# Two states of each unit take their product with B on GpSimd, and three positions per unit change who makes it

## What is computed

```python
dt = jax.nn.softplus(jnp.einsum('blr,dr->bld', x_dbl[..., :DT_RANK], dt_w) + dt_b)
Bm = x_dbl[..., DT_RANK:DT_RANK + D_STATE]
Cm = x_dbl[..., DT_RANK + D_STATE:]
dA = jnp.exp(dt[..., None] * A)
dBu = dt[..., None] * Bm[:, :, None, :] * u[..., None]
def step(h, ins):
    dA_t, dBu_t, C_t = ins
    h = dA_t * h + dBu_t
    y = jnp.einsum('bdn,bn->bd', h, C_t)
    return (h, y)
```

## Time and profile before

| | |
|---|---|
| median of 3 runs | 503.31 us |
| the profiled execution | 503.27 us, its span 501.5 us |
| first scan starts, last scan starts | 29.7 us, 466.3 us |
| busy: DVE, PE, ACT, POOL | 436.4, 421.1, 374.1, 370.7 us |
| scans (DVE) | 128, 290.4 us busy |
| products with B (DVE) | 92, 111.7 us busy |
| products with C (POOL) | 129, 301.2 us busy |
| mean granted TensorE clock | 0.912 of full speed |

### The profile page before, as it was taken

The page is one execution under the profiler, slowest core; times in us unless marked ns, Lnnn a source line. Parts: engine busy times, 40 slices in busy tenths (PEclk is TensorE's granted clock), DMA queues, the critical chain, the costliest instruction groups (busy, mean ns, idle before and its releaser), DMA issues.

```text
span 501.5 us, 6592 instructions
## 1 busy us (share of the span) xinstructions
PE 421.1 (84%) x2236; PEld 279.5 (56%) x2236; DVE 436.4 (87%) x357; ACT 374.1 (75%) x716; POOL 370.7 (74%) x226
## 2 busy tenths in 40 slices
PE   1947985999689897989899879999998977989754
PEld 1335654665445494555555676655645665558543
DVE  4577877999999987999999897999999788999454
ACT  2398799679959778999689786998687788684140
POOL 1799769577977797879688877878677977866521
PEclk9957988899999799999999797998999597799878
DMA  7242212212221222221122221222222122110001
GB/s 241 80 168 67 91 58 84 83 78 94 79 89 56 91 69 85 84 88 59 72 81 105 88 85 53 75 86 85 84 71 94 72 84 84 58 68 2 0 1 42
DMA packets 14721, 39.28 MB, mean 78 GB/s; under 512 B 1376, under 2 KB 5728, under 8 KB 14688
## 3 DMA queue, kind: packets, MB, share of 16 engines
q1 hardware_dynamic: 14688, 38.87, 22.2%
HBM read 37.55 MB, written 1.31 MB: 77 GB/s over the span
## 4 chain that ended last, share of the span: by engine, by line
DVE 24%; PE 24%; issue 20%; POOL 10%; ACT 7%; POOLq 0%; DVEq 0%; ACTq 0%
DVE bb L1072 11%; DVE hq L1084 10%; POOL hq L977 9%; PE ysum L618 8%; PE scr L729 3%; PE bb L599 3%; PE scr L697 2%; ACT da L784 2%; PE scr L660 2%; ACT g L871 2%; PE bb L572 1%; PE scr L750 1%; PE bb L750 1%; PE scr L555 1%; ACT ln_tile L888 1%
## 5 line engine op out<-in xcount | busy, mean ns | idle before, releaser
L977 POOL TENSOR_TENSOR hq<-hq,c_tiles 128x1024 f32<-128x1024 f32 x129 | 301.2, 2347 | 86.5 <-DVE hq L1084 86.5
L1084 DVE TENSOR_TENSOR_SCAN hq<-da,bb 128x1024 f32<-128x1024 f32 x128 | 290.4, 2281 | 22.3 <-PE bb L599 18.9
L784 ACT ACTIVATE da<-dt,neg_a 128x511 f32<-128x511 f32 x256 | 167.0, 712 | 24.2 <-DVE hq L1084 23.9
L618 PE MATMUL ysum<-wts,hq 128*128 128x128 f32 x1024 | 149.2, 293 | 4.3 <-POOL hq L977 4.1
L618 PEld LDWEIGHTS ysum<-wts,hq 128*128 128x128 f32 x1024 | 122.0, 149 | 28.9 <-issue 21.1
L1072 DVE TENSOR_TENSOR bb<-bb,dtu 128x1024 f32<-128x1024 f32 x92 | 111.7, 1214 | 8.8 <-PE bb L572 5.3
L871 ACT ACTIVATE g<-dtu_t,bc_t 128x256 f32<-128x256 f32 x144 | 61.0, 497 | 0.0
L599 PE MATMUL bb<-wts,g 128*128 128x128 f32 x288 | 41.8, 292 | 20.9 <-ACT g L871 19.5
L599 PEld LDWEIGHTS bb<-wts,g 128*128 128x128 f32 x288 | 34.3, 149 | 37.6 <-ACT g L871 23.5
L572 PE MATMUL bb<-b_rows,pick 48*128 48x512 bf16 x88 | 35.7, 406 | 16.0 <-DVE hq L1084 15.3
L572 PEld LDWEIGHTS bb<-b_rows,pick 48*128 48x128 bf16 x88 | 8.2, 94 | 52.9 <-DVE hq L1084 32.7
(11 more groups left out here) (123 smaller groups left out, 430.6 us busy)
## 6 DMA issues: line engine op xcount, KB each, us to landing
c_tiles<-c_rows_dram SPq DMA_DIRECT2D x64, 512.0 KB, 3.5
wconv<-conv_taps_dram SPq DMA_DIRECT2D x2, 512.0 KB, 7.3
x_res<-x_dram SPq DMA_DIRECT2D x1, 768.0 KB, 9.1
out_dram<-o SPq DMA_DIRECT2D x3, 256.0 KB, 2.3
wts<-packed_dram SPq DMA_DIRECT2D x1, 584.0 KB, 10.1
ffn_stage<-w_ffn_dram SPq DMA_DIRECT2D x1, 576.0 KB, 8.5
wts<-packed_dram SPq DMA_DIRECT2D x1, 437.0 KB, 7.0
x_res<-x_dram SPq DMA_DIRECT2D x1, 256.0 KB, 2.9
```

The costliest lines, as they stand in the source:

```text
L618: mm = nc.tensor.matmul(ysum[:, h, block(b)], hq[:, i % H_RING, h, block(b)], ident, start=(first and b == 0), stop=(i % NS == NS - 1), is ...
L784: ins = nc.scalar.activation(da[:, i % DA_RING, h, 1:SEQ], dt[:, k % 2, h, 1:SEQ], ACT.Exp, scale=neg_a[:, c:c + 1])
L977: nc.gpsimd.tensor_tensor(hq[:, i % H_RING, halves, :], hq[:, i % H_RING, halves, :], c_tiles[:, n % C_RING, i % 2, :].unsqueeze(1).broadc ...
L1084: nc.vector.tensor_tensor_scan(out=hq[:, i % H_RING].rearrange("p h t -> p (h t)"), data0=da[:, i % DA_RING].rearrange("p h t -> p (h t)") ...
```

## The change

A third kind of step is added, **pooled**, at positions 8 and 15 of a unit (15 alone in unit 0), 15 steps in all. Its dBu is made on POOL (stage "mul_b_pooled"): `dtu` times a row of B that SP has loaded, broadcast over the partitions, into `b_tiles` (a ring of 2, 256 KB per transfer). The result goes to `dbu`, one tile in SBUF. It is put behind mul_c of position 4 (for 8) and of position 12 (for 15), and waits for the scan of the last pooled step. For such a step ACT writes the decay not into `da` but into the `bb` tile in PSUM (stage "exp_psum"): one copy of the two zero columns and two exp instructions. This stage stands where the bcast of the step would stand, one slot ahead of the scan, and waits for scan i - 2, where the exp into `da` stood five slots ahead. The scan of the step reads the decay from PSUM and dBu from SBUF.

The table TURNED has other positions (33 turned steps in place of 36), so 80 plain steps are left of 92. The copies "g" are placed by a table, 3 to 5 slots ahead in place of 3; in the forward units from 2 on, dtu_turn and the "g" of the next unit's position 0 move one slot earlier. The buffer in DRAM now holds the rows of B too (32 rows per unit in place of 16). The staging tile for the feed-forward weights shares the memory of `hid`.

```diff
-TURNED = ((4, 6, 8, 10, 12, 14), (0, 3, 6, 9, 11, 13)) + 3 * ((6, 9, 12, 14), (0, 6, 9, 13))
+TURNED = ((4, 6, 10, 13), (0, 4, 6, 10, 13)) + 3 * ((3, 6, 10, 13), (0, 5, 10, 13))
+POOLED = ((15,),) + 7 * ((8, 15),)
+POOLED_RING = 2
...
+        g_slot = {3: 0, 4: 1, 5: 1, 6: 2, 10: 6, 13: 8 if ffn else 10}
         for p in TURNED[k]:
             if p:
-                put(at + p - 3, ("g", at + p))
+                put(at + g_slot[p], ("g", at + p))
+        for p in POOLED[k]:
+            put(at + {8: 4, 15: 12}[p], ("mul_b_pooled", at + p))
...
-            put(at + 12, ("dtu_turn", n, 0))
-            put(at + 13, ("dtu_turn", n, 1))
+            soon = 1 if d == 0 and k >= 1 else 0
+            put(at + 12 - soon, ("dtu_turn", n, 0))
+            put(at + 13 - soon, ("dtu_turn", n, 1))
...
-                put(at + 14, ("g", at + NS))
+                put(at + 14 - soon, ("g", at + NS))
...
-        return [("exp", n) for n in ahead.get(i, (i + DA_RING - 1,)) if n < STEPS]
+        return [("exp", n) for n in ahead.get(i, (i + DA_RING - 1,)) if n < STEPS and not is_pooled(n)]
...
-                order.append(("g_turn" if is_turned(i + 1) else "bcast", i + 1))
-            if i + 1 < STEPS and not is_turned(i + 1):
+                order.append(("g_turn" if is_turned(i + 1) else "exp_psum" if is_pooled(i + 1) else "bcast", i + 1))
+            if i + 1 < STEPS and not is_turned(i + 1) and not is_pooled(i + 1):
                 order.append(("mul_b", i + 1))
...
-                sp.dma_start(c_rows[k], xdbl[ROW_C:ROW_C + NS, :]).then_inc(s_cst, 16)
+                sp.dma_start(bc_rows[k], xdbl[0:2 * NS, :]).then_inc(s_cst, 16)
...
+                    for p in POOLED[k]:
+                        if m == {8: 0, 15: 3}[p]:
+                            n = pooled_steps(NS * k + p)
+                            if n >= POOLED_RING:
+
+                                sp.wait_ge(s_dbu_pooled, n - POOLED_RING + 1)
+                            sp.dma_start(b_tiles[:, n % POOLED_RING], bc_rows[k, ROW_B + p].partition_broadcast(P)
+                                         ).then_inc(s_bl[n % POOLED_RING], 16)
...
+                elif stage == "exp_psum":
+
+                    i, = a
+                    k, n = i // NS, i % NS
+                    act.wait_ge(s_scan, i - BB_RING + 1)
+                    nc.scalar.activation(bb[:, i % BB_RING, :, 0:1], da[:, 0, :, 0:1], ACT.Copy)
+                    for h in range(2):
+                        c = (2 * (k % 2) + h) * NS + n
+                        ins = nc.scalar.activation(bb[:, i % BB_RING, h, 1:SEQ], dt[:, k % 2, h, 1:SEQ],
+                                                   ACT.Exp, scale=neg_a[:, c:c + 1])
+                    ins.then_inc(s_exp_psum, 1)
...
+                elif stage == "mul_b_pooled":
+
+                    i, = a
+                    k, n = i // NS, pooled_steps(i)
+                    dtu_ready(pool, k)
+                    pool.wait_ge(s_bl[n % POOLED_RING], 16 * (n // POOLED_RING + 1))
+                    if n >= 1:
+                        last = next(j for j in range(i) if pooled_steps(j + 1) == n)
+                        pool.wait_ge(s_scan, last + 1)
+                    nc.gpsimd.tensor_tensor(dbu[:], dtu[:, k % 2],
+                                            b_tiles[:, n % POOLED_RING].unsqueeze(1).broadcast_to([P, 2, SEQ]),
+                                            ALU.mult).then_inc(s_dbu_pooled, 1)
...
+                    decay, dbu_tile = da[:, i % DA_RING], bb[:, i % BB_RING]
+                    if is_pooled(i):
+                        decay, dbu_tile = bb[:, i % BB_RING], dbu
```

More of the change, by code:

```diff
@@ L73, in is_turned, with is_pooled, turned_steps, pooled_steps @@
     return i % NS in TURNED[i // NS]
+def is_pooled(i):
+    return i % NS in POOLED[i // NS]
+def turned_steps(i):
+    return sum(is_turned(n) for n in range(i))
+def pooled_steps(i):
+    return sum(is_pooled(n) for n in range(i))
 def plain_steps(i):
-    return sum(not is_turned(n) for n in range(i))
-def turned_steps(i):
-    return i - plain_steps(i)
+    return i - turned_steps(i) - pooled_steps(i)
 def from_rows(i):
@@ L91, in first_from_rows @@
 def first_from_rows(k):
-    return next(i for i in range(NS * k, NS * k + NS) if from_rows(i) and not is_turned(i))
+    return next(i for i in range(NS * k, NS * k + NS) if from_rows(i) and not is_turned(i) and not is_pooled(i))
 def parts_of(q):
@@ L280, in plan_banks, with mamba_sandwich @@
     return banks
-def mamba_sandwich(nc, x, packed, conv_taps, w_u, w_ffn, c_rows, out):
+def mamba_sandwich(nc, x, packed, conv_taps, w_u, w_ffn, bc_rows, out):
     ORDER = plan()
@@ L303, in mamba_sandwich @@
         skip_diag = sb("skip_diag", [P, 2, 2, P])
-        ffn_stage = sb("ffn_stage", [P, 3 * HID], I32)
         wffn = sb("wffn", [P, 3 * HID])
@@ L344, in mamba_sandwich @@
         c_tiles = sb("c_tiles", [P, C_RING, 2, SEQ])
+        b_tiles = sb("b_tiles", [P, POOLED_RING, SEQ])
+        dbu = sb("dbu", [P, 2, SEQ])
         y_t = sb("y_t", [P, 2, SEQ])
@@ L348, in mamba_sandwich @@
         hid = sb("hid", [P, 3, SEQ])
+        ffn_stage = hid.rearrange("p c t -> p (c t)")[:, 0:3 * HID].bitcast(I32)
         def col(name):
@@ L385, in mamba_sandwich @@
         s_exp = sem("da_done")
+        s_exp_psum = sem("da_in_psum_done")
+        s_bl = [sem(f"b_tile{n}_loaded") for n in range(POOLED_RING)]
+        s_dbu_pooled = sem("pooled_dbu_done")
         s_scan = sem("scan_done")
@@ L522, in _ @@
             sp.dma_start(wconv[:, 1], conv_taps[:, 1]).then_inc(s_wc[1], 16)
-            sp.dma_start(ffn_stage[:], w_ffn).then_inc(s_wf, 16)
+            sp.dma_start(ffn_stage, w_ffn).then_inc(s_wf, 16)
             for k in range(UNITS):
                 was_read(sp, ("xproj", k))
-                sp.dma_start(c_rows[k], xdbl[ROW_C:ROW_C + NS, :]).then_inc(s_cst, 16)
+                sp.dma_start(bc_rows[k], xdbl[0:2 * NS, :]).then_inc(s_cst, 16)
                 sp.wait_ge(s_cst, 16 * (k + 1))
@@ L535, in _ @@
                     sp.dma_start(c_tiles[:, n % C_RING].rearrange("p s t -> p (s t)"),
-                                 c_rows[k, 2 * m:2 * m + 2].rearrange("s t -> (s t)").partition_broadcast(P)
+                                 bc_rows[k, ROW_C + 2 * m:ROW_C + 2 * m + 2].rearrange("s t -> (s t)"
+                                                                                      ).partition_broadcast(P)
                                  ).then_inc(s_cl[n % C_RING], 16)
+                    for p in POOLED[k]:
[5 more added lines that the diff above has]
+                                         ).then_inc(s_bl[n % POOLED_RING], 16)
                     if m == 5 and k >= 4 and k % 2 == 0:
@@ L1001, in _ @@
                     pool.wait_ge(s_wf, 16)
-                    nc.gpsimd.tensor_scalar(wffn[:], ffn_stage[:], 1.0 / 127.0, None, ALU.mult).then_inc(s_wffn, 1)
+                    nc.gpsimd.tensor_scalar(wffn[:], ffn_stage, 1.0 / 127.0, None, ALU.mult).then_inc(s_wffn, 1)
                 elif stage == "split":
@@ L1024, in _ @@
                         pool.wait_ge(s_dbu, plain_steps(NS * (k - 1)))
+                        pool.wait_ge(s_dbu_pooled, pooled_steps(NS * (k - 1)))
                         for h in range(2):
@@ L1076, in _ @@
                     i, = a
-                    if is_turned(i):
-                        dve.wait_ge(s_g_turn, turned_steps(i) + 1)
-                    else:
-                        dve.wait_ge(s_dbu, plain_steps(i) + 1)
-                    dve.wait_ge(s_exp, i + 1)
+                    if is_pooled(i):
+                        dve.wait_ge(s_dbu_pooled, pooled_steps(i) + 1)
+                        dve.wait_ge(s_exp_psum, pooled_steps(i) + 1)
+                    else:
+                        dve.wait_ge(s_exp, i - pooled_steps(i) + 1)
+                        if is_turned(i):
+                            dve.wait_ge(s_g_turn, turned_steps(i) + 1)
+                        else:
+                            dve.wait_ge(s_dbu, plain_steps(i) + 1)
                     if i >= H_RING:
                         dve.wait_ge(s_fold, i - H_RING + 1)
+                    decay, dbu_tile = da[:, i % DA_RING], bb[:, i % BB_RING]
+                    if is_pooled(i):
+                        decay, dbu_tile = bb[:, i % BB_RING], dbu
                     nc.vector.tensor_tensor_scan(out=hq[:, i % H_RING].rearrange("p h t -> p (h t)"),
-                                                 data0=da[:, i % DA_RING].rearrange("p h t -> p (h t)"),
-                                                 data1=bb[:, i % BB_RING].rearrange("p h t -> p (h t)"), initial=0.0,
+                                                 data0=decay.rearrange("p h t -> p (h t)"),
+                                                 data1=dbu_tile.rearrange("p h t -> p (h t)"), initial=0.0,
                                                  op0=ALU.mult, op1=ALU.add).then_inc(s_scan, 1)
@@ L1250 @@
```

(2 more changed lines are left out.)

## The result

| | before | after |
|---|---|---|
| median, us | 502.94 (4 runs, 501.96 to 504.02) | 496.28 (4 runs, 493.99 to 498.06) |
| ratio | | 0.9857, 95% interval 0.9822 to 0.9892 |
| profiled execution: span | 501.5 | 494.3 |
| first scan starts, last scan ends | 29.7, 468.6 | 29.7, 458.5 |

A forecast was written before the change was run, and what follows sets the result against it. DVE was taken to pace the steps, with PE the next bound. The terms -15.0 - 12.0 + 7.2 + 1.5 summed to -18.3 us, from 503.27 to 485.0 us, range 473 to 498.

The forecast's parts named there:

- DVE's work, -15.0 us: DVE's plain steps: 92 become 80, so 12 products with B leave at 1.25 us each, -15.0 us.
- The turned products, -12.0 us: DVE's waits for PE's turned products: -8.9 us at position 0, -2.5 at position 12, -0.6 in unit 0.
- The exp of a pooled step, +7.2 us: ACT's exp one step ahead: late 2.4 us at position 15 of units 2, 4, 6; about in time at position 8.
- POOL and PE, +1.5 us: POOL's lag from 15 more products and PE without slack: cover thin, +1.5 us over the whole, ends 0 and 14.
- The tail: Time behind the last scan: 32.9 us, claimed unchanged.
- rival 2: All waits go, late exp costs nothing, PE holds 2.4 GHz longer: -27 us, 476.3 us; chance 0.12.
- rival 1: PE and POOL take the pace, PE keeps 4.3 us idle per unit: -5.6 us, 497.7 us; chance 0.17.
- The rule of the Trainium skill: Elementwise work on two tensors belongs on VectorE: the 15 pooled products would lose 17 us of engine time.
- Rival 3: Slower: exp of pooled steps late everywhere in ACT's queue, 3.0 us each, +18 us, 521 us; chance 0.06.

The follow-up runs named there:

- a_all3_short: a_all3 with POOL's product for pooled steps cut to 16 of 512 columns per half, so it computes something else: ratio 0.9605 to the kernel before, 484.3 us.
- n_all3: a_all3 without pooled steps: ratio 0.9739 to the kernel before, 489.5 us.
- b_soon: Kernel before, only dtu_turn and the g of the next unit's position 0 one slot earlier in units 2, 4, 6: ratio 0.9786, 492.4 us.
- a_all3: Changed kernel with the scan's wait for the decay last again, g of position 10 and copy o one slot later: ratio 0.9683 to the kernel before, 489.1 us.
- a_wait_order: Changed kernel with the scan's wait for the decay again behind its wait for the product: ratio 0.9776 to the kernel before, 491.6 us.
- a_short_product: Changed kernel with POOL's product for pooled steps cut to 16 of 512 columns per half, a measure only: ratio 0.9757 to the kernel before, 491.5 us.

## Why the prediction was wrong in size

**DVE's work, -15.0 us ("Nothing covers them, DVE was running without a gap where they stood").** This is the step that failed. The products left (80 remain, 97.0 us) and the scans stayed at 2.29, but the time off DVE isn't time off the kernel: 16.7 us of it brought 6.7 where the products cost POOL next to nothing (a_all3_short against n_all3). With all that comes with them, the 15 pooled steps lengthened the kernel, by 1.1% on the old table and 0.9% on the new. That an engine runs without a gap shows that it paces these steps now; it doesn't say by how much it is ahead of the next. I had that number, PE 50.2 and POOL 48.8 us per unit against 49.3 of DVE, called the cover thin, and priced it at 1.5 us.

**The turned products, -12.0 us.** The mechanism and its place were right. Its main term, 8.9 us for position 0 of units 3, 5, 7, is 10.8 us by b_soon (9 to 13 by its interval; 8.7 us less waiting for turned products in its trace). In the changed kernel these waits are 2.6 us in all, not the 7 that I named: the half that I had left at position 12 went, but for 0.7 us of waiting for a broadcast, and the wait at position 0 of unit 1, which was to stay at 3.7, fell to 2.0.

**The exp of a pooled step, +7.2 us.** At position 15 three waits of 2.4 were forecast and three of 2.09 came. "At position 8 I find ACT in time or nearly so" was wrong: five waits, 5.3 us, behind the g of position 10 (unit 3: g from 215.21, exp ready 218.19). Its own length was right to 0.1 us (0.16 for the zero columns, which is less than the smallest that I had found, and 1.29). So the term was 11.6 us of waiting where 7.2 were forecast. Putting the exp in time brought some 4.7 us (a_all3 against a_wait_order), less than the waits that went.

**POOL and PE, +1.5 us.** Undersized: POOL's products alone cost 5 us (a_short_product). The path starts as I had worked it out and found to "just fit": mul_c late, PE's fold late (17.0 us of waiting where it was 4.1). Yet POOL lagged less than I had said: mul_c ends 3.7 us behind its scan on average and more than 5 in 30 of 127 steps (2.9 us and 12 steps before), not 5 to 7 over most of a unit. The last link, the broadcast late for DVE, is 5.8 us of waits in all, 5.3 before, so how PE's waiting becomes time of the kernel is argued and not shown. The tail, "unchanged" in the forecast, took 2.9 us more.

**Not seen:** the order of the two waits, about 4 us in this kernel (a_wait_order), some 2 in the two others. I had read that hunk of the diff and priced nothing.

The three repairs together (a_all3_short against the changed kernel, 2.5% or 12.7 us) are about as large as the 11.6 us between forecast and result. That match is luck. The forecast already held 8.7 us for the exp and for POOL (7.2 and 1.5), so with both repaired its own sum is rival 2's, -27 us or 476.3, and 484.3 were measured, with 4 us of waits for the exp left. Split up, the 15 products off DVE were to bring 15 x 1.25 = 18.8 us and brought 6.7; the rest of the change, without pooled steps, was to bring 12.0 less three products, 8.3 us, and brought 13.1 (n_all3). The two errors have opposite signs.

Of the rivals, the first was nearest, 497.7 against 496.3, and its mechanism is in the trace: PE kept its idle time, 4.8 us per unit in units 3 to 6 where it was to stay at 4.3, with waits for late products with C in place of waits for late copies. Its work was 48.5 us and not 50.2, so these units last 53.3 us on average, where rival 1 had 54.5 and the forecast 52 to 53; the rest of the shortfall is in unit 7 and in the tail. That PE is the next bound behind DVE fits this, but no run makes PE's work lighter, so which engine takes back the time stays open.

The rule of the Trainium skill that was weighed there (GPSIMD Engine Reference, "Engine selection") came out right for this change as it stands: moving the products made the kernel slower. The ratio of the two products is as the page says, 2369 ns against 1213; the loss came by POOL's place in the chain and by the waits that came with the pooled steps. Rival 3's mechanism was at work at eight sites of 15 but short of its price, 11.6 us where 27 would have used up the gain.

## What to carry to other kernels

When the engine that sets the pace has neighbours within a few per cent of it, a microsecond taken off it is worth far less than a microsecond: here 0.4, and less than nothing once the work had to be done by a neighbour. Compare the engines' busy times per stage after the edit before you price it. A wait of several microseconds that comes once per unit, from one item standing late in another engine's order, is the better target: here three numbers in the order brought 2.1%, while a new kind of step with a ring of tiles, four semaphores and 15 DMAs lost 0.9%. When an operand loses its lead (here from five steps to one), list everything that stands ahead of it on its engine at each site, not only at the one that looks worst.
